# Unnormalised attention outputs with a separate scale row, and a new step table, in a two-layer transformer on one core

## What is computed

```
xn = layernorm(x); x = x + lightning_attention(xn) + block_sparse_ffn(xn)
xn = layernorm(x); x = x + rope_attention(xn) + fp4_ffn(xn)

# rope_attention, the part that the change is mostly in; 8 key heads, 32 query heads, width 64
scores = q @ k.T / 8, causal, over 1024 tokens of each of 2 sequences
attn = softmax(scores); out = (attn @ v) @ o_w.T
```

## Time and profile before

| | us |
|---|---|
| median of 3 runs (lowest, highest) | 2313.44 (2312.14, 2317.91) |
| the profiled execution | 2313.69 |
| its span, first to last instruction | 2311.9 |
| PE busy, DVE busy, ACT busy, POOL busy | 2077.5, 1544.6, 874.0, 486.2 |
| mean granted TensorE clock | 0.972 |

### The profile page before, as it was taken

One profiled execution on the slowest core, in us unless ns is written; L12 is line 12 of the kernel. 1 busy time (PEld: TensorE's weight loads), 2 busy tenths in 40 slices (PEclk: granted clock), 3 DMA queues, 4 the chain that ended last, 5 costly groups with the idle time before them and its releaser, 6 DMA issues. The chain is left out here.

```text
span 2311.9 us, 54178 instructions
## 1 busy us (share of the span) xinstructions
PE 2077.5 (90%) x22192; PEld 1468.3 (64%) x22192; DVE 1544.6 (67%) x2534; ACT 874.0 (38%) x1836; POOL 486.2 (21%) x408
## 2 busy tenths in 40 slices
PE   7999969999988999778888888888888699999997
PEld 5777758877766788634444444444444588787776
DVE  6544423799966354478989988889998330477776
ACT  4222123222213200045655655565665221234443
POOL 0111112222310145401111111111111444221111
PEclk9999989999998999979999999999999899999999
DMA  5122154344326533333443333343332555320101
GB/s 179 56 93 75 38 195 151 109 134 132 121 94 250 177 121 121 110 77 84 102 106 99 93 100 87 84 113 107 92 92 77 214 170 183 111 90 19 55 1 37
DMA packets 197121, 251.26 MB, mean 109 GB/s; under 512 B 38496, under 2 KB 119712, under 8 KB 194208
## 3 DMA queue, kind: packets, MB, share of 16 engines
q1 hardware_dynamic: 196032, 247.85, 34.7%
q10 hardware_dynamic: 864, 0.21, 0.0%
HBM read 165.08 MB, written 82.90 MB: 107 GB/s over the span
## 5 line engine op out<-in xcount | busy, mean ns | idle before, releaser
L1614 ACT ACTIVATE a_prob<-ps,a_nmax 128x256 f32<-128x256 f32 (+7 forms) x512 | 377.4, 739 | 349.4 <-DVE a_nmax L1642 211.2
L1727 PE MATMUL ps<-a_kt,a_q 64*128 64x512 f32 (+5 forms) x1536 | 380.4, 536 | 85.3 <-ACT a_prob L1614 63.6
L1642 DVE TENSOR_REDUCE a_nmax<-ps 128x1 f32<-128x1024 f32 (+3 forms) x256 | 256.1, 1000 | 73.0 <-PE ps L1727 71.5
L1659 DVE STREAM_TRANSPOSE a_pt_long<-a_prob 128x512 f32<-128x512 f32 (+3 forms) x512 | 278.1, 580 | 0.0
L1727 PEld LDWEIGHTS ps<-a_kt,a_q 64*128 64x128 f32 x1536 | 143.1, 193 | 184.5 <-ACT a_prob L1614 116.7
L1741 PE MATMUL ps<-a_pt_long,a_v 32*64 32x256 f32 (+3 forms) x7808 | 228.6, 344 | 2.5 <-issue 1.0
L2021 DVE SCALAR_TENSOR_TENSOR f_part<-ps,f_gu_scale,f_part 128x512 f32<-128x512 f32 x264 | 184.6, 745 | 65.8 <-PE ps L2068 52.5
L1741 PEld LDWEIGHTS ps<-a_pt_long,a_v 32*64 32x64 f32 x7808 | 153.9, 132 | 105.1 <-issue 77.1
L1694 POOL TENSOR_TENSOR a_o<-a_left 128x256 f32<-128x256 f32 x128 | 90.3, 726 | 595.5 <-ACT a_left L1624 595.5
L940 POOL TENSOR_TENSOR f_hT_lo<-f_h,f_hT_hi 128x512 fp32r<-128x512 f32 x64 | 89.7, 1407 | 294.5 <-ACT f_hT_hi L923 294.5
L1724 PE MATMUL ps<-a_causal,a_identb 64*128 64x128 bf16 x1024 | 112.2, 224 | 39.5 <-ACT a_prob L1614 39.5
(11 more groups left out here) (228 smaller groups left out, 4552.4 us busy)
## 6 DMA issues: line engine op xcount, KB each, us to landing
a_q<-scratch_QT SPq DMA_DIRECT2D x512, 64.0 KB, 2.1
scratch_QT<-k_qo SPq DMA_DIRECT2D x64, 256.0 KB, 2.3
a_v<-scratch_V SPq DMA_DIRECT2D x64, 256.0 KB, 4.3
scratch_OT<-a_o SPq DMA_DIRECT2D x32, 512.0 KB, 3.4
o_of<-scratch_OT SPq DMA_DIRECT2D x32, 512.0 KB, 4.1
f_block<-in_packed SPq DMA_DIRECT2D x33, 256.0 KB, 3.4
f_mask<-scratch_maskT SPq DMA_DIRECT2D x16, 512.0 KB, 5.1
a_kt<-scratch_KT SPq DMA_DIRECT2D x128, 64.0 KB, 4.2
```

The lines of the kernel that those rows point to most:

```text
L1614: last = nc.scalar.activation(prob[:, n % PRING, s].rearrange("p (a w) -> p a w", w=w), SC[n % 2][:, a, 0:w], ACT.Exp, bias=nmax[:, n % 4, ...
L1642: nc.vector.tensor_reduce(nmax[:, n % 4, 0:1], SC[n % 2][:, :, 0:width(0, t)], AX.XY, ALU.max, negate=True).then_inc(maxed, 1)
L1659: last = nc.vector.transpose(pt[hf][:, lo:hi, h, t - FIRST[hf], :], src.rearrange("p (j k) -> p j k", k=32))
L1727: last = pe.matmul(sc[:, a, 0:w], q[r, slot, heads[a * hf], :], kt[r, b, keys], start=not masked, stop=True, skip_group_check=True)
```

## The change

- feed_forward0: PE goes through the blocks one at a time, each over the four token tiles, and waits for one more `h_lo` ahead of each. `y_done` comes in the last block.
- projections1: `eps` and `ident` are loaded first under a semaphore of their own, on which ACT and PE start; then the four weights, then the four rotation tables.
- attention1: no denominators on PE, no work on POOL. ACT evicts the plain sums to `o` (two instructions a half, two banks each), SP stores them. DVE inverts once a unit, turns the 32 columns (L1682), and SP stores them to a new scratch `R` in four small DMAs. `pt_long` is doubled and cut at 24 blocks, the last 8 in `pt_wide`. Short values come first (steps 26 to 30), then the long ones (34 to 46). Every transpose is two steps late. Rings: `q` 3 in place of 4, `prob` 4 in place of 8.
- output1: rows of `R` are broadcast into `rd` by two DMAs of 64 partitions a step, DVE multiplies (a new 128x1024 instruction a step), then ACT and POOL as before. Step 0 is done in two pieces of 512 columns.

```diff
@@ feed_forward0, PE
-                        for bs in (range(BPQ - 2), range(BPQ - 2, BPQ)):
-                            pe.wait_ge(h_lo.sem, h_lo.now(it, bs[-1] + 1))
+                        for b in range(BPQ):
+                            pe.wait_ge(h_lo.sem, h_lo.now(it, b + 1))
                             for t in range(TPC):
...
@@ projections1
-                act.wait_ge(c_in.sem, ALL_CONSTS)
+                act.wait_ge(first_in.sem, 32)
...
-                pe.wait_ge(c_in.sem, ALL_CONSTS)
+                pe.wait_ge(first_in.sem, 32)
@@ attention1
-QRING = 4
-PRING = 8
+QRING = 3
+PRING = 4
...
-LONG_VALUES = {18 + i: range(3 * i, 3 * i + 3) for i in range(10)}
-SHORT_VALUES = {31 + i: range(2 * i, 2 * i + 2) for i in range(8)}
+SHORT_VALUES = {26: range(0, 3), 27: range(3, 6), 28: range(6, 9), 29: range(9, 13), 30: range(13, 16)}
+LONG_VALUES = {34: range(0, 2), 35: range(2, 4), 36: range(4, 6), 37: range(6, 8), 38: range(8, 10), 39: range(10, 11),
+               40: range(11, 13), 41: range(13, 15), 42: range(15, 18), 43: range(18, 21), 44: range(21, 24),
+               45: range(24, 28), 46: range(28, 32)}
+SHORT_LEFT = {31: (0,), 32: (1,)}
+LONG_LEFT = {47: (0, 1)}
...
-                        nc.scalar.activation(left[:, i].rearrange("p w s t q -> p (w s t q)"), PV[i], ACT.Copy
+                        nc.scalar.activation(
+                            o[:, i % 2, :, :, 2 * k:2 * k + 2, :].rearrange("p s t i q -> p i (s t) q"),
+                            PV_ALL[:, 2 * k:2 * k + 2, 0:256].rearrange("p i (w q) -> p i w q", q=32), ACT.Copy
...
+                            near = min(blocks, MAIN)
+                            last = nc.vector.transpose(pt_long[:, unit % 2, 0:near, h, t - 4, :], src[:, 0:near, :])
+                            if blocks > MAIN:
+                                last = nc.vector.transpose(pt_wide[:, unit % 2, 0:blocks - MAIN, h, t - 6, :],
+                                                           src[:, MAIN:blocks, :])
...
-                            last = pe.matmul(PV[i][c * HD1:(c + 1) * HD1, 256:512], ones[rows, :],
-                                             spread[rows, c::2, :, :], start=True, stop=True, skip_group_check=True)
@@ output1
+                        for a in range(2):
+                            sp.dma_start(rd[a * HD1:(a + 1) * HD1, n % 2, s],
+                                         d["R"][k // 2, b, 2 * (k % 2) + a, s].partition_broadcast(HD1)
+                                         ).then_inc(landed(n, i), 16)
...
+                        nc.vector.tensor_tensor(of[:, n % 3, s], of[:, n % 3, s], rd[:, n % 2, s], ALU.mult
+                                                ).then_inc(scaled, 1)
```

More of the change, by code:

```diff
@@ L1565, in load_v @@
                     g, b = divmod(u, NB1)
[L1566 removed]
+                    wait(sp, valued, 2 * u - 2)
                     for i in range(4):
@@ L1646, in maxima, with turn @@
                                                 negate=True).then_inc(maxed, 1)
-                def turn(n, part):
+                def turn(n):
                     unit, hf, t, heads = place(n)
-                    if n % USTEPS == 0 and part == FRONT:
-                        wait(dve, half_valued, unit)
-                    elif n % USTEPS in (0, LONG):
-                        wait(dve, valued, 2 * unit + hf - 1)
+                    if n % USTEPS == 0:
+                        wait(dve, valued, order(unit - 2, 0) + 1)
+                    elif n % USTEPS == LONG:
+                        wait(dve, valued, order(unit - 1, 1) + 1)
@@ L1661, in turn @@
-                    last.then_inc(turned, 1)
-                def invert(u, hf):
-                    half = 2 * u + hf
-                    dve.wait_ge(exped, u * USTEPS + (LONG, USTEPS)[hf])
-                    wait(dve, spread_out, half)
-                    nc.vector.reciprocal(rden[:], den[:, hf, :]).then_inc(inverted, 1)
+                        src = prob[:, n % PRING, i * blocks * 32:(i + 1) * blocks * 32]
+                        src = src.rearrange("p (j k) -> p j k", k=32)
+                        if hf:
+                            last = nc.vector.transpose(pt_short[:, 0:blocks, h, t, :], src)
+                        else:
+                            near = min(blocks, MAIN)
[3 more added lines that the diff above has]
+                                                           src[:, MAIN:blocks, :])
@@ L1669, in _, with invert @@
+                    last.then_inc(turned, 1)
+                def invert(u):
+                    dve.wait_ge(exped, (u + 1) * USTEPS)
+                    nc.vector.reciprocal(rden[:], den[:, u % 2, :]).then_inc(inverted, 1)
+                    dve.wait_ge(inverted, u + 1)
+                    wait(dve, r_stored, 64 * u)
+                    nc.vector.transpose(rdenT[:], rden[:]).then_inc(r_turned, 1)
                 for n in range(NSTEPS + LATEST):
@@ L1733, in value_block @@
                     t0, b, k = FIRST[hf], unit % NB1, j // 4
+                    part, p0 = turned_part(unit, hf, j)
                     for c in range(2):
@@ L2153, in constants @@
     }
-    tables["c_ones"] = np.ones((P, HD1))
-    tables["c_diag32"] = np.tile(np.eye(32), (4, 1))
     tables = {k: v.astype(f32) for k, v in tables.items()}
```

223 lines of the change are left out of this document (102 added, 121 removed).

## The result

The changed kernel took 2291.93 us (median of six runs, 2287.1 to 2299.76) beside 2313.31 (2311.39 to 2317.91) of the kernel before on the same chip: a ratio of 0.9906, 95% interval 0.9883 to 0.9929. It is faster by 21 us, not by 62, and 2292 lies above the range of 2234 to 2276. The profiled executions are 2289.46 and 2313.69 us, with spans of 2287.6 and 2311.9.

What follows compares the result with a forecast made beforehand. In attention1 neither PE nor DVE alone was the bound; a unit sums the longer of both per step. -2.7 - 7.2 - 2.8 - 5 - 50 + 6 - 0.5 = -62.2 from 2313.69 gave 2251 us, range 2234 to 2276.

Steps and rivals of the forecast that it cites:

- The signs of being wrong: Named in advance: an attention1 unit staying above 48.5 us, PE waiting in output1, or the clock falling in steady units.
- output1, -0.5: output1: multiplies hidden from PE, first step in pieces saves slightly more than it costs; -0.5 us, between -1.5 and +10.
- Rival D: output1: multiply and POOL instructions wait for each other, a step of 6.1 us; kernel 2262 to 2266 us, chance 0.12.
- Units 1 to 15, -50: attention1: summing the longer of PE and DVE per step gives 46.6 us a unit against 49.9; -50 us.
- Rival B: attention1: the clock falls to 0.50 for 17 us in every unit, +8.5 us each; kernel slower, 2378 us, chance 0.04.
- Unit 0, -5: attention1's first unit: no value products, scores alone at half clock, 46 us against 51.1; -5, between -1 and -8.
- Behind the last score, +6: End of attention1 to output1: more value blocks left, 27.7 us against 21.7; +6, between +4 and +8.
- Start of attention1, -2.8: Start of attention1: the first score no longer waits for `ones`, only for the earlier `causal`; -2.8, between -2 and -4.
- Start of projections1, -7.2: Start of projections1: ACT's root no longer waits 7.8 us for the last table; -7.2 us, between -5 and -7.8.
- feed_forward0, -2.7: feed_forward0: PE stands one block, 2.7 us, further ahead of DVE when unpacking ends; -2.7, between 0 and -6.4.
- Rival C: attention1: PE's lead evens the steps out and DVE alone binds, 43.9 us a unit; kernel 2210 us, chance 0.07.
- E: attention1: the waits add up, 48 us a unit, +21; kernel 2272 us, chance 0.13.

Runs made afterwards that it cites:

- o1_rd_plain128: Changed kernel with output1's spread rows of R replaced by plain OT rows in one 128-partition transfer (wrong scale values): 2269.27 us, ratio 0.9792 to the kernel before.
- o1_rd_twice: Changed kernel with the spread rows of `rd` loaded only for output1's first two steps, all multiplies kept: 2273.7 us, ratio 0.9807 to the kernel before.
- a1_fill: Changed kernel with one more 384-column filling matmul ahead of the score in steps 7 to 9 of each attention1 unit: 2273.43 us, ratio 0.9812.
- the last version: Changed kernel with POOL scaling in attention1, old output1, both short-half evictions in step 7, long blocks from step 9, filling matmuls also in unit 0: 2249.82 us.
- before_of_halves: Kernel before with o_of's 512 KB loaded as two transfers of 64 partitions in place of one of 128: 2317.17 us, ratio 1.001.
- o1_rd_one: Changed kernel with output1's two spread rows of a step in one transfer over 128 partitions, not two over 64: 2531.1 us, ratio 1.0942.

## Why the prediction was wrong

The signs of being wrong that the prediction named came: PE waits in output1, the clock falls in steady units, and the units with a fall take 48.5 us or more.

- **output1, -0.5, measured +22: the step that failed.** It priced 32 multiplies and "about 1 for the loads" of the first step, and never set the new loads against the DMA's room, though the earlier trace rows had the share at 0.51. 16.8 MB more at the old 159 ns a packet make 0.76 (o1_rd_plain128), still under the room; the halves of 64 partitions make 0.93 and the loads late. The bound of +10 came from DVE and POOL, which were not the cause (o1_rd_twice). That a multiply can be stretched to POOL's length is borne out by ten multiplies there, and so is that PE sees none of it. Rival D, output1 starves, had the right effect and the wrong mechanism.
- **Units 1 to 15, -50, measured -33.5: the sum per step was right, the clock was not.** At full clock a unit takes 46.5 us (forecast 46.6), and a1_fill shows the whole: 701.4, which is -49.2. Missing are the falls at step 10. Rival B named that place and gave it 0.04, on the ground that 8.5 us with 5.8 busy stand at clock 1.00 in the earlier trace rows. But that row is not the like of steps 7 to 9 after the change, with 2.03 busy of 3.9 and the dense steps right behind them. B's price was wrong as well: falls of 3.4 or 6.8 us in half of the units, not of 17 in all, so that it took a third of the gain and left the sign.
- The rule of the Trainium skill that the prediction cited for B (TensorE: Matmul & The Clock Gate, section "A second HAM failure mode: psum-queue depth-cycling") was set aside because no row of steady units agreed. Of the changed kernel's units 1 to 15, eight do.
- **Unit 0, -5, measured -2.7:** right in kind, but with 28 us of half clock in it where 17 were counted on. In the last version, where the filling takes most of that away, the unit takes 46.1 us, beside 46 forecast.
- **Behind the last score, +6, measured +5.9;** 27.2 us from the last score's end to output1's first load, 27.7 forecast.
- **Start of attention1, -2.8, measured -2.6. Start of projections1, -7.2, measured -7.0:** ACT's wait for the table is gone, and what ends last is now DVE. **feed_forward0, -2.7, measured -4.0:** PE's waits of the earlier trace rows are now

```profile
PE ps L50 <- POOL f_hT_lo L940: 2.5, 5, 0.5
```

so 3.9 of the 6.4 us were gain, more than the one block counted.
- Rival C fell (DVE alone does not bind), and E (the waits add up) as well: no unit at full clock takes 48.

## What to carry to other kernels

A new load is to be priced twice: its bytes and its shape against the share of the DMA that the stage has left, before anything else of it is counted. Ask of each stretch where PE isn't the longer one how idle it gets, since the clock of the next stretch, where it is, can hang on it; a useless matmul there was worth 15.7 us here, 0.7%. And work that moves to an engine with nothing to do, in a stage whose DMA is half idle, costs only its last latency.

## What the runs showed of the hardware

- Two transfers of 64 partitions in place of one of 128, same bytes and rows: a 4096-byte packet 208 ns in place of 159, share 0.64 in place of 0.51 (before_of_halves).
- One transfer with an outer dimension of two and 64 copies in each: share 0.34, one load of 512 KB in each step of 13.2 us (o1_rd_one).
- 2.03 us busy of 3.9 before a dense stretch (changed kernel): falls to 0.50 for 3.4 or 6.8 us in eight of 15 units; 3.21 of 3.9 (a1_fill): none.
- DVE's 1024-element multiply with two SBUF operands took 1.2 us where no subtraction of POOL ran, and 1.9 to 3.3 us in ten of the 14 that one overlapped (o1_rd_twice). wo_lo, 512 elements, began within 0.5 us of a subtraction in most steps and took 2.43 at the median, 0.69 alone (changed kernel).
